# Four buffers in place of three for the gathered LoRA matrix A, with its loads one place earlier in SyncE's queue

## What is computed

```
W0 = L0_cond_weights[itok_B_0_15]
x  = x + einsum('bct,bcd->bdt', x, W0)

base = einsum('bti,oi->bto', x, W) + b
h    = einsum('bti,bir->btr', x, lora_As[itok_B_0_23])     # rank 16
x    = x + base + 2 * einsum('btr,bro->bto', h, lora_Bs[itok_B_0_23])
```

## Time and profile before

| what | value |
|---|---|
| median of 3 runs | 84.2 us (84.03 to 84.33) |
| the profiled execution's own time | 84.65 us |
| its span | 82.9 us |
| PE busy | 79.0 us (95%) |
| DVE, ACT, POOL busy | 60.1, 52.3, 34.0 us |
| granted TensorE clock | full in every slice |
| HBM traffic | 192 GB/s over the span |

### The profile page before, as it was taken

The page is one execution under the profiler, slowest core; times in us unless marked ns, Lnnn a source line. Parts: engine busy times, 40 slices in busy tenths (PEclk is TensorE's granted clock), DMA queues, the critical chain, the costliest instruction groups (busy, mean ns, idle before and its releaser), DMA issues.

```text
span 82.9 us, 2011 instructions
## 1 busy us (share of the span) xinstructions
PE 79.0 (95%) x524; PEld 71.7 (86%) x524; DVE 60.1 (72%) x158; ACT 52.3 (63%) x179; POOL 34.0 (41%) x75
## 2 busy tenths in 40 slices
PE   4999999999998999999999999999999999999970
PEld 2377987999997999999999999999999999999950
DVE  2059875987859787777778787888787777869560
ACT  1547729687746676868676766666685857665520
POOL 6108864753533527062715344352618071304300
PEclk9999999999999999999999999999999999999999
DMA  0999887874965679888488796775668726030334
GB/s 15 288 365 301 198 261 188 234 213 108 307 132 204 205 203 265 320 211 250 120 239 214 250 240 212 172 259 160 156 221 235 229 76 179 19 124 0 126 126 127
DMA packets 16142, 16.07 MB, mean 194 GB/s; under 512 B 10242, under 2 KB 10627, under 8 KB 16131
## 3 DMA queue, kind: packets, MB, share of 16 engines
q1 hardware_dynamic: 14016, 11.67, 48.3%
q0 software_dynamic: 1248, 4.06, 17.0%
q10 hardware_dynamic: 866, 0.21, 1.1%
HBM read 11.74 MB, written 4.19 MB: 192 GB/s over the span
## 4 chain that ended last, share of the span: by engine, by line
PE 76%; SPq 8%; DMA 6%; issue 3%; DVE 3%; ACT 1%; DVEq 0%
PE z_ps L572 45%; PE z_ps L609 8%; DMA x_raw<-in_xt 6%; SPq L237 5%; PE ht_ps L563 5%; PE z_ps L652 4%; PE y_ps L624 3%; PE y_ps L620 3%; PE y_ps L622 3%; PE ht_ps L596 2%; PE ht_ps L661 1%; DVE y_sb L557 1%; SPq L234 1%; ACT x_hi L360 1%; SPq L236 1%
## 5 line engine op out<-in xcount | busy, mean ns | idle before, releaser
L572 PE MATMUL z_ps<-wa,x_hi 128*128 128x288 f32 (+2 forms) x240 | 50.2, 301 | 0.0
L572 PEld LDWEIGHTS z_ps<-wa,x_hi 128*128 128x128 f32 x240 | 38.0, 188 | 1.9 <-issue 0.5
L572 PE MATMUL z_ps<-wa,x_lo 128*128 128x288 f32 (+2 forms) x120 | 35.2, 295 | 0.0
L572 PEld LDWEIGHTS z_ps<-wa,x_lo 128*128 128x128 f32 x120 | 22.5, 188 | 0.0
L311 POOL CAST m_hi<-m_raw 128x128 fp32r<-128x128 f32 x16 | 4.8, 303 | 34.8 <-ACT m_raw L348 34.8
L302 POOL DMA_INDIRECT b_raw<-in_lora_b,b_index_slot x16 | 17.3, 1081 | 4.4 <-POOL b_index_slot L300 4.4
L492 DVE TENSOR_TENSOR z_lo<-z_ps,z_hi 128x256 fp32r<-128x256 f32 x31 | 11.8, 420 | 6.1 <-ACT z_hi L392 6.1
L392 ACT CAST z_hi<-z_ps 128x256 fp32r<-128x256 f32 x31 | 10.2, 376 | 9.1 <-PE z_ps L609 9.1
L348 ACT COPY m_raw<-w_raw 32x32 f32 x64 | 13.8, 216 | 1.9 <-issue 1.2
L451 DVE TENSOR_TENSOR x_lo<-x_raw,x_hi 128x512 fp32r<-128x512 f32 x14 | 9.6, 689 | 4.0 <-ACT x_hi L360 4.0
L472 DVE TENSOR_TENSOR b_lo<-b_raw,b_hi 128x512 fp32r<-128x512 f32 x15 | 10.4, 692 | 0.6
(11 more groups left out here) (57 smaller groups left out, 76.8 us busy)
## 6 DMA issues: line engine op xcount, KB each, us to landing
out<-y_sb SPq DMA_DIRECT2D x15, 256.0 KB, 3.2
x_raw<-in_xt SPq DMA_DIRECT2D x14, 256.0 KB, 3.3
a_raw<-in_lora_a SPq DMA_DIRECT2D x60, 32.0 KB
first_sb<-in_first SPq DMA_DIRECT2D x2, 384.0 KB, 3.8
first_sb<-in_first SPq DMA_DIRECT2D x3, 256.0 KB, 4.5
b_raw<-in_lora_b,b_index_slot POOLq DMA_INDIRECT x16, 4.1
bias_sb<-in_bias SPq DMA_DIRECT2D x1, 256.0 KB, 3.5
a_raw<-in_lora_a ACTq DMA_DIRECT2D x4, 32.0 KB
```

The lines of the kernel that those rows point to most:

```text
L572: done = nc.tensor.matmul(target, (x_hi, x_lo)[part[0]][u % 2][:, k, :], moving(part[1]), start=k == 0 and part == HH, stop=k == KC - 1 an ...
```

## The change

A gets a fourth buffer, and one more load of A stands ahead of the loop.

```diff
     NX = 3
-    NA = 3
+    NA = 4
     NB = 3
...
             load_x(4)
+            load_a(NA)
             for u in range(1, TILES):
                 if u + NA < TILES:
                     load_a(u + NA)
```

## The result

The changed kernel takes 85.37 us in the median of 22 runs, the kernel before 84.41 in as many; the ratio is 1.0096, with a 95% interval of 1.0074 to 1.0118. Medians are over all runs, while the ratios, here and in the experiments, compare runs in the faster of two states alone, which leaves out four of these 22 runs of the changed kernel, one of the six of experiment 2 and five of the twelve of experiment 6. The forecast was 84.1 with a range up to 85.1, so the time lies outside it, on the side of the second rival. The profiled execution took 85.42 us (before: 84.65).

A forecast was written before the change was run, and what follows sets the result against it. PE was taken as the bound, busy 79.0 of 82.9 us, with 0.63 us of stalls to gain. x5 landing at 24.1 against 24.20 gains 0.1, so 84.2 becomes 84.1; range 83.95 to 84.45, 8 in 10 83.5 to 85.1.

The forecast's parts named there:

- the second rival: Instruction fetch holds x5 on one DMA engine, landing at 24.45 to 25.5; lora(3) 0.25 to 1.3 us later; chance 30%.
- The reference: Two long PE steps of the first profile, 0.63 us too much together, and x5's landing at 24.20 as baseline.
- the first part: What bounds the kernel: PE waits only in two long steps, 0.14 and 0.49 us, so 0.63 is about the most.
- step 5: On PE, lora(3) starts 2.0 us behind x5's landing; total changes by landing minus 24.20; gain 0.1 us.
- Step 3: In SyncE's queue, one more load of A, 2.45 us, precedes x5; issued at 20.8 in place of 19.51.
- Step 1: In SyncE's queue, A3 no longer waits for PE's read of A0 and starts 1.02 us earlier; later waits cost nothing.
- Step 2: At ScalarE, A3 lands at about 14.7, not 15.69, so lora(1) starts on time, taking away 0.14 us.
- signs of being wrong: x5 out before 20, a step after the fifth longer than 4.5, or PE waiting for A anywhere.
- Step 4: x5's load takes the median 3.3 us and lands at 24.1, against 24.20 before; bounds 23.5 and 26.0.
- Its floor of -0.63: Limit in the rule for the total: the change can never gain more than the two long steps' 0.63 us.
- Step 6: Later loads: x6 goes out between 23.6 and 25.4, lands by 28.7, wanted at 28.6; cost taken as nothing.
- The rule of the Trainium skill: DMA time of 2.0 us plus bytes over 436 GB/s; x5 would land at 23.4, total 83.6; not used.

The follow-up runs named there:

- experiment 2: Changed kernel with the wait ahead of A3 for the matmuls of tile 0 kept, so only the load order changes; 86.05 us, ratio 1.0147.
- experiment 6: Changed kernel with the gather of B2 sent behind the split of the first mixing matrix, some 3 us later; 85.77 us, ratio 1.0100.
- experiment 7: Changed kernel with five buffers and a second load of A ahead of the loop, so two more loads precede x5 than before; 91.34 us, ratio 1.0832.
- experiments 1 to 7: Seven edited kernels, built on the changed one, varying the order, number or wait of loads, or when B2 is gathered; ratios 0.9984 to 1.0832.

## Why the prediction was wrong, point by point

- **The reference, in the first part and step 5, failed.** The forecast took the two long steps of one profile as what the kernel loses, and measured x5's landing against 24.20. In two more profiles of the same kernel nothing is lost. The load of x5 that took 4.69 us, against a median of 3.3, was a long one (in the other two profiles it was there within 4.2 and 3.5 us), and I set my forecast of a *normal* load for the changed kernel (3.3) against this *long* one of the kernel before. The apparent 1.4 us of faster landing offset the 1.3 us of later sending, and "no change" came out. With 3.3 on both sides x5 lands at 22.8 before, a microsecond ahead of the 23.86 at which ScalarE is free, and at 24.1 after, 0.4 behind the 23.7 of step 5: a loss of 0.4 us, where the forecast had a gain of 0.1.
- **Step 3 was mis-sized, and that is the larger part.** 20.94 was counted and is right (21.01 where nothing was held). I took 20.8: the 0.34 us of "issue" that I half dropped is there in the changed kernel too, as a row of 0.39 at 18.06, ahead of A6. And I had no term for a held transfer, though the row for A6, 3.65 us for four transfers, showed that such a thing happens. It cost 0.98 and 1.13 us in the two profiles of the changed kernel.
- **Together** the 0.4 and the 0.98 come to about the 1.37 us that the first profile of the changed kernel has over 67.15. The medians are 0.96 apart. Before, the time moves with the first mix (15.13 was the earliest of three); in the changed kernel x5 goes out at 21.91 and 22.02 with the first mix at 15.17 and 15.58. That this is the rest of the difference is argued, not shown. Another 0.2 us of the miss is the base: three runs of the kernel before gave 84.2, 22 runs gave 84.41.
- **Step 1** was right: A3 went out at 10.28 against 10.21, and no later wait showed. **Step 2** was wrong in one profile (A3 at 16.19, the step 5.07 in place of 4.48, so that PE waited for A, one of the prediction's own signs of being wrong) and right in the other (no idle for A3); the second profile and experiment 6 show that it does not count, as both are as slow with A3 in time.
- **Step 4** was right in its value, 3.3 against 3.08 and 3.15 measured.
- **Step 5's rule held.** Between the two first profiles the landing of x5 moved by 24.99 - 24.20 = 0.79, and the span by 0.8. Its floor of -0.63 is the reference's mistake again: there was hardly anything to gain.
- **Step 6 held in what it concludes**: x6 went out at 25.35 and was in time, and no step behind the one with lora(3) is longer than in a kernel where nothing waits. Its count was 0.5 us short: from y0 to x6, with no transfer of A7 held, it has 2.4 us, and the changed kernel took 2.96 (22.39 to 25.35), because A7's first transfer goes out a microsecond behind y0.
- **The rivals.** The size of the second one (0.25 to 1.3 us later) came true, but not its way: x5 was not long on its way, it was sent late. If a fetch had a part in it, it was in the *sending* of A6.
- **The rule of the Trainium skill** (DMA: Bandwidth & Descriptors, "Anatomy of one DMA"), by which 2.6 us was the estimate for such a load, is for one on GpSimd's path. No load of x5, sent by SyncE, that PE waited for in these runs was that fast; the chains have 3.08, 3.09, 3.15, 3.57, 3.71 and 4.69.

What stays open: how often a transfer of A6 is held (in both profiles of the changed kernel, not in experiments 2 and 6), and why the last of A3's rows came so late in the first.

## What to carry to other kernels

A buffer more does not speed up a queue that is issued in order: the load that it lets out early stands in front of the load that is needed first. Count, for each consumer, the time from sending to need, and change the order only where the transfer that is moved has more of it than the ones it passes. And before a stall of half a microsecond in one profile is called the gain to be had, look at whether the load in it took its usual time; if it did not, forecast from the usual one on both sides.

## What the runs showed of the hardware

**SyncE's sending of a transfer can be held while an instruction fetch is on a DMA engine.** In the changed kernel the held one ran from 20.56 to 21.87, beside a fetch of about 1.25 us. In the kernel before, the last transfer of A6 held until 24.54, beside the fetch of the earlier trace rows:

```profile
23.34 1.20 SPq L237 DMA_DIRECT2D a_raw<-in_lora_a  x1
```

Others take 0.33. In the twelve profiles all 31 transfers that SyncE took over 0.8 us to send overlap a fetch. But a fetch alone is not enough: in experiment 6 one of 1.01 us ran from 18.52 to 19.53, and the transfer of A6 that SyncE sent at 19.05 took 0.34. No run took a fetch away, so that the one causes the other is argued, not shown.

**PE's loop starts up to a microsecond earlier or later from run to run** with the same program (first mix at 15.13, 15.38 and 16.10 in three profiles of the kernel before). The old wait ahead of A3 ties SyncE's queue to PE: from the second to the third profile of the kernel before the first mix moved by 0.72 us, and x4's sending by 0.73 (13.90 to 14.63). Without that wait x4 is sent between 12.6 and 12.8 whatever PE does.

**A wait of 4 us on PE cost 2.6 us more through the clock** (experiment 7). The stalls of 0.5 to 1.7 us in the other runs were followed by steps of 4.5 us in their profiles. All four runs of experiment 7 show a mean granted clock of 0.962. Two of the 22 runs of the changed kernel (87.80 and 87.95 us) and two of the twelve of experiment 6 (88.36 and 88.21) show 0.980, and none of the 52 runs of the kernel before that ran beside experiments 1 to 7 shows less than 0.994. So the late x5 may at times cost the changed kernel its clock as well; these runs have no trace, and that is not shown.
